# Reordering the stages of a recommendation-tower kernel: lookups three further ahead, small banks first in each quarter, 37 gathered rows, four one-hot chunks, and another place where gathers start

## The reference: what is computed

```python
e = jnp.stack([tbl_0[ids[:, 0]], ..., tbl_25[ids[:, 25]]], axis=1)
combined = jnp.concatenate([dense[:, None, :], e], axis=1)         # 2048 x 27 x 128
pairs = jnp.einsum('bfd,bgd->bfg', combined, combined)[:, I, J]    # upper triangle, 351
h = jnp.concatenate([dense, pairs, dense], axis=1)                 # 607
h = jnp.maximum(h @ W_top1 + b_top1, 0.0)                          # 512
h = jnp.maximum(h @ W_top2 + b_top2, 0.0)                          # 256
y = h @ W_top3                                                     # 1
```

## Time and profile before

| | |
|---|---|
| timed runs, median (lowest, highest) | 520.17 us (515.14, 522.70) |
| profiled execution, its own time | 515.3 us |
| its span, first to last instruction | 513.2 us |
| mean granted TensorE clock | 0.88 of full |
| TensorE matmul busy | 408.8 us, 80% of the span |
| VectorE, ScalarE busy | 262.7 us, 208.7 us |
| GpSimd busy | 254.1 us, 50% |

### The profile page before, as it was taken

The page is one execution under the profiler, slowest core; times in us unless marked ns, Lnnn a source line. Parts: engine busy times, 40 slices in busy tenths (PEclk is TensorE's granted clock), DMA queues, the critical chain, the costliest instruction groups (busy, mean ns, idle before and its releaser), DMA issues.

```text
span 513.2 us, 14192 instructions
## 1 busy us (share of the span) xinstructions
PE 408.8 (80%) x6280; PEld 365.9 (71%) x6280; DVE 262.7 (51%) x323; ACT 208.7 (41%) x436; POOL 254.1 (50%) x265
## 2 busy tenths in 40 slices
PE   5886727777978598875978788887989689789977
PEld 4776716767878497764967687785878588778755
DVE  3789505654555554663553655655364655454220
ACT  3456302234343543444342553435243543337432
POOL 5778875551555555552555535553555535540000
PEclk8998857776999898988897978997898969899989
DMA  6994251230322222221222212221232212210000
GB/s 170 227 240 107 67 158 50 70 108 23 74 59 78 56 64 68 69 64 32 64 66 70 63 49 64 67 74 49 68 68 69 63 42 70 58 39 1 4 1 0
DMA packets 27972, 36.34 MB, mean 71 GB/s; under 512 B 9151, under 2 KB 21959, under 8 KB 27912
## 3 DMA queue, kind: packets, MB, share of 16 engines
q1 hardware_dynamic: 19704, 18.65, 14.6%
q0 software_dynamic: 8192, 16.79, 13.5%
q10 hardware_dynamic: 16, 0.01, 0.0%
HBM read 35.42 MB, written 0.01 MB: 69 GB/s over the span
## 4 chain that ended last, share of the span: by engine, by line
PE 71%; issue 13%; ACT 4%; SPq 4%; DMA 4%; DVE 2%; another core or an unknown queue 1%; ACTq 0%; DVEq 0%
PE ring L411 17%; PE ring L412 15%; PE gram L449 10%; PE ring L485 8%; PE ring L431 7%; PE ring L494 6%; DMA dense<-in_r_dense_features 4%; PE ring L483 3%; SPq L281 2%; PE ring L461 2%; PE ring L472 2%; DVE pairs_and_more L674 2%; PE ring L503 2%; ACT pairs_and_more L578 1%; SPq L275 1%
## 5 line engine op out<-in xcount | busy, mean ns | idle before, releaser
L359 POOL DMA_INDIRECT rows<-in_tbl,ids_all x256 | 248.7, 971 | 201.1 <-PE gram L449 127.3
L651 DVE TENSOR_TENSOR onehot<-idb,vrow 125x1024 fp32r<-125x1024 f32 x160 | 192.7, 1222 | 130.5 <-PE ring L412 58.7
L411 PE MATMUL ring<-onehot,table_hi 125*128 125x256 f32 x608 | 181.6, 328 | 22.1 <-DVE pairs_and_more L674 7.6
L412 PE MATMUL ring<-onehot,table_lo 125*128 125x256 f32 x608 | 169.5, 309 | 0.0
L411 PEld LDWEIGHTS ring<-onehot,table_hi 125*128 125x128 f32 x608 | 132.9, 219 | 28.8 <-issue 8.7
L412 PEld LDWEIGHTS ring<-onehot,table_lo 125*128 125x128 f32 x608 | 133.4, 219 | 0.8
L559 ACT COPY xt<-ring 128x256 f32<-128x256 f32 x80 | 54.2, 677 | 128.9 <-PE ring L412 68.3
L449 PE MATMUL gram<-xt 128*27 128x26 f32 x4096 | 55.1, 201 | 42.6 <-issue 40.0
L449 PEld LDWEIGHTS gram<-xt 128*27 128x27 f32 x4096 | 47.8, 114 | 51.7 <-issue 46.0
L567 ACT COPY xt<-ring 128x512 f32<-128x512 f32 (+1 forms) x56 | 51.2, 987 | 24.1 <-remote 16.0
L431 PE MATMUL ring<-ident,rows 128*128 128x128 f32 x256 | 38.6, 285 | 13.6 <-issue 6.7
(11 more groups left out here) (41 smaller groups left out, 209.7 us busy)
## 6 DMA issues: line engine op xcount, KB each, us to landing
ids_spread<-in_ids_t SPq DMA_DIRECT2D x70, 128.0 KB
rows<-in_tbl,ids_all POOLq DMA_INDIRECT x256
xt<-in_tbl SPq DMA_DIRECT2D x6, 448.0 KB
w<-in_tbl SPq DMA_DIRECT2D x3, 448.0 KB
rows<-in_ids_t SPq DMA_DIRECT2D x10, 128.0 KB, 5.7
dense<-in_r_dense_features SPq DMA_DIRECT2D x16, 64.0 KB
w<-in_W_top SPq DMA_DIRECT2D x4, 256.0 KB
w<-in_W_top SPq DMA_DIRECT2D x1, 512.0 KB
```

Source lines behind the costliest of these rows:

```text
L359: pool.indirect_dma_start(rows[:, i % ROWS, :], None, aps[f"tbl_{f}"], bass.IndirectOffsetOnAxis(ap=ids_all[:, k, f:f + 1].bitcast(U32), a ...
L411: pe.matmul(ps, table_hi[:, m, c * KC + k, :], chosen, start=first, stop=False)
L412: last = pe.matmul(ps, table_lo[:, m, c * KC + k, :], chosen, start=False, stop=final)
L651: dve.tensor_tensor(onehot[:, (CH * u + c) % SLOTS], idb[0:VP, u % 2, 0:BS].unsqueeze(1).to_broadcast([VP, KC, BS]), vrow[:, c * KC:(c + 1 ...
```

## The change

The order of `stages()` is new. The lookups of block n + 1 now begin in the fourth quarter of block n - 1 (three of them), so they are three further ahead. Unblock and pairs of block n move out of its fourth quarter into the first two quarters of block n + 1, the layers follow them later, and the two tiles' rows are spread over the quarters with the first two banks of a next tile a quarter earlier. In each quarter the small banks stand ahead of most lookups. The copies of `gram` are a stage of their own ("grams"), with the engines exchanged. Pairs take two banks instead of three and layer 1 two instead of four. There are four one-hot slots in place of three, and VectorE makes one-hots one lookup further ahead; ScalarE lays out ids three ahead. `rows` has 37 places instead of 45, which is the same memory as the fourth slot. The rows of the first tile of a block are all stored by ScalarE.

A group of gathers from the fourth on waits for the bank that stands just ahead of a product step (`TURNS`), not for the end of the step before it. The two lower parts on GpSimd stand one group earlier. The first block's ids come in one DMA of ten rows and are spread by TensorE with a matmul (`spread_first_ids`); the first two dense tiles are loaded behind the fourth and the seventh table.

```diff
-ROWS = 45
+ROWS = 37
-    SLOTS = 3
+    SLOTS = 4
@@ stages()
+        yield "first_ids", 0, 0, 0
+        yield "first_ids", 0, 1, 0
+        for m in range(NL - 1):
+            if m + 2 < NL:
+                yield "first_ids", 0, m + 2, 0
+            yield from lookups(0, m)
+        yield from rows(0, 0, 0, 1, 2, 3, 4)
         yield from lookups(0, NL - 1)
         for n in range(NB):
             yield "products", n, 0, 0
+            yield from layer("unblock", n - 1, 0, 1)
+            yield from lookups(n + 1, *([0, 1, 2] if n == 0 else [3]))
+            yield from layer("unblock", n - 1, 2, 3)
+            yield "grams", n, 0, 0
+            yield from layer("layer3", n - 2, 0)
+            yield from rows(n, 1, 0, 1)
+            yield from lookups(n + 1, *([3] if n == 0 else [4, 5]))
+
+            yield "products", n, 1, 0
+            yield "grams", n, 1, 0
+            yield from layer("pairs", n - 1, 0, 1)
+            yield from lookups(n + 1, *([4, 5] if n == 0 else [6]))
+            yield from rows(n, 1, 2, 3, 4)
+            yield from layer("layer1", n - 1, 0)
+            yield from lookups(n + 1, *([6] if n == 0 else [7]))
+
+            yield "products", n, 2, 0
+            yield "grams", n, 2, 0
+            yield from layer("layer1", n - 1, 1)
+            yield from lookups(n + 1, *([7] if n == 0 else []))
+            yield from rows(n + 1, 0, 0, 1)
+            yield from lookups(n + 1, 8, 9)
+
+            yield "products", n, 3, 0
+            yield "grams", n, 3, 0
+            yield from layer("layer2", n - 1, 0)
+            yield from rows(n + 1, 0, 2, 3, 4)
+            yield from lookups(n + 2, 0)
             if n == NB - 1:
+                yield from layer("unblock", n, 0, 1)
+            yield from layer("layer2", n - 1, 1)
+            yield from lookups(n + 2, 1, 2)
+        yield from layer("unblock", NB - 1, 2, 3)
+        yield from layer("layer3", NB - 2, 0)
+        yield from layer("pairs", NB - 1, 0, 1)
+        yield from layer("layer1", NB - 1, 0, 1)
...
+    RING_ORDER = [stage for stage in stages() if stage[0] in RING_STAGES + ("products",)]
+    TURNS = [stage_ahead for stage_ahead, stage in zip(RING_ORDER, RING_ORDER[1:]) if stage[0] == "products"]
-        return g == 1 or (t, g) == (1, 3)
+        return t == 1 and g in (1, 3)
-    FIRST_GROUPS_BEHIND = {1: 0, 2: 3, 3: 6, 4: 9}
+    FIRST_GROUPS_BEHIND = {1: 0, 2: 3, 3: 6}
@@ SP
+            sp.dma_start(first_ids_i, aps["ids_t"][:, 0:BS]).then_inc(first_ids_landed, 16)
             for m in range(NL):
-                spread_ids(m)
                 load_raw(m)
-            load_dense(0)
-            load_dense(1)
+                if m in (3, 6):
+                    load_dense(m // 4)
@@ GpSimd
-                    pool.wait_ge(gram_ready, group - 4)
+                    pool.wait_ge(ring_filled, filled(*TURNS[group - 4]))
...
+                    if (k, g) == (1, GROUP):
+                        for m in LO_ON_GPSIMD:
+                            lower_part(m)
@@ TensorE
+            def spread_first_ids(m):
+                if m == 0:
+                    pe.wait_ge(first_ids_ready, 1)
+                if m >= 2:
+                    pe.wait_ge(onehot_ready, CH * (m - 1))
+                pe.matmul(idb[0:VP, m % 2, 0:BS], ident[0:NL, m:m + 1].to_broadcast([NL, VP]), first_ids, start=True,
+                          stop=True).then_inc(first_idb_ready, 1)
@@ VectorE
+                if s == 0 and n > 0:
+                    dve.wait_ge(ring_filled, filled("unblock", n - 1, NU - 1, 0))
                 dve.tensor_copy(*product_views(s)).then_inc(gram_dve, 1)
...
-                        one_hot(u, 0)
-                        ...
-                        one_hot(u, 1)
+                    if u + 1 < NB * NL:
+                        one_hot(u + 1, 0, 1)
```

More of the change, by code:

```diff
@@ L97, in stages @@
[L97 to L106, removed]
-            if n == NB - 1:
-                yield from layer("layer2", n - 1, 0)
-            yield "products", n, 2, 0
@@ L193, in build @@
         y_row = beside_pairs[:, 0:BS]
[L195 to L203, removed]
+        first_ids_i = pairs_and_more[0:NL, 0, 0:BS].bitcast(I32)
+        first_ids = pairs_and_more[0:NL, 1, 0:BS]
         W = KT * D
@@ L218, in build @@
         ids_landed = sem("ids_landed")
-        first_ids_landed = [sem(f"first_ids_landed{m}") for m in range(NL)]
+        first_ids_landed = sem("first_ids_landed")
+        first_ids_ready = sem("first_ids_ready")
+        first_idb_ready = sem("first_idb_ready")
         ids_spread_landed = [sem(f"ids_spread_landed{q}") for q in range(IDS_SLOTS)]
@@ L510, in _ @@
             for stage, n, a, b in stages():
-                if stage == "lookup":
+                if stage == "first_ids":
+                    spread_first_ids(a)
+                elif stage == "lookup":
                     lookup(n, a)
@@ L579, in store_unblocked, with store_pairs, store_layer1, store_layer2 @@
                 last.then_inc(left("unblock", n, b, 0), 1)
-            def store_pairs(n, k):
-                w = K_PAIR[k][1]
-                ps = bank("pairs", n, k, 0)
-                act.copy(x[0:w, k, :], ps[0:w, 0:BS]).then_inc(left("pairs", n, k, 0), 1)
-            def store_layer(stage, n, b, h_next, bias):
-                ps = bank(stage, n, b, 0)
-                act.activation(h_next[:, b, :], ps[:, 0:BS], ACT.Relu, bias=bias[:, b:b + 1]).then_inc(left(stage, n, b, 0), 1)
+            def store_pairs(n, b):
+                ps = bank("pairs", n, b, 0)
+                k, w = (slice(0, 2), P) if b == 0 else (slice(2, 3), K_PAIR[2][1])
+                act.copy(x[0:w, k, :].rearrange("p k s -> p (k s)"), ps[0:w, 0:(k.stop - k.start) * BS]).then_inc(
+                    left("pairs", n, b, 0), 1)
+            def store_layer1(n, b):
+                ps = bank("layer1", n, b, 0)
+                for i in range(2):
+                    block = 2 * b + i
+                    last = act.activation(h1[:, block, :], ps[:, i * BS:(i + 1) * BS], ACT.Relu, bias=b1[:, block:block + 1])
+                last.then_inc(left("layer1", n, b, 0), 1)
+            def store_layer2(n, b):
+                ps = bank("layer2", n, b, 0)
+                act.activation(h2[:, b, :], ps[:, 0:BS], ACT.Relu, bias=b2[:, b:b + 1]).then_inc(left("layer2", n, b, 0), 1)
             def store_y(n):
@@ L603, in _ @@
             act.copy(x[:, 0, 0:P], ident[:])
+            act.wait_ge(first_ids_landed, 16)
+            act.copy(first_ids, first_ids_i).then_inc(first_ids_ready, 1)
             act.wait_ge(pads_cleared, 1)
-            for m in (0, 1):
-                lay_out_ids(m)
-                upper_part(m)
+            upper_part(0)
+            upper_part(1)
             for stage, n, a, b in stages():
                 if stage == "lookup":
-                    if n * NL + a + 2 < NB * NL:
-                        lay_out_ids(n * NL + a + 2)
+                    if NL <= n * NL + a + 3 < NB * NL:
+                        lay_out_ids(n * NL + a + 3)
                     if n == 0 and a + 2 < NL:
@@ L616, in _ @@
                     store_rows(n, a, b)
-                elif stage == "products" and a % 2 == 0:
+                elif stage == "grams" and a % 2 == 1:
                     store_products(n, a)
@@ L699, in _ @@
                     store_unblocked(n, a)
-                elif stage == "products" and a % 2 == 1:
+                elif stage == "grams" and a % 2 == 0:
                     store_products(n, a)
```

102 lines of the change are left out of this document (38 added, 64 removed).

## The result

| | before | after |
|---|---|---|
| timed runs, median (lowest, highest) | 518.75 us (515.14, 522.70), 4 runs | 753.30 us (752.83, 754.25), 4 runs |
| ratio, 95% interval | | 1.457 (1.450 to 1.464) |
| profiled execution, its span | 515.3, 513.2 us | 754.25, 752.4 us |
| TensorE busy; mean granted clock | 408.8 us, 80%; 0.88 | 512.0 us, 68%; 0.76 |

The changed kernel is 46% slower; the forecast was 445 us, range 412 to 495. Times depend on the chip: on the chip of this comparison, and on two chips of later runs, the kernel before took about 520 us, on three others 404 to 408. None of the later chips was met a second time, so whether a chip always belongs to its kind, or was only in a state of that kind, is not shown.

A forecast was written before the change was run, and what follows sets the result against it. The prediction took TensorE's order and its unexplained idle time, with product steps stalled by gathers, as the bound. First block 105, six blocks 291 and last 45 made 441 us of span; 445 us predicted, range 412 to 495.

The forecast's parts named there:

- The step that failed: Product step starting with a group of gathers: expected to get through undisturbed, 1.2 us inside a quarter of 11.6 us.
- the drain: Behind a group's last gather issue: product step goes on 1.6 us later; rival with 2.5 us gave 462, chance 0.10.
- The work of the quarters: A block's four quarters: 12.4 us for the first with VectorE, then 10.5, 9.4 and 11.6 of TensorE work.
- The unblock chain: Unblock, copies and pairs at a block's end: now costs nothing, with lookups and the product step between its banks.
- The ring of 37: Places for gathered rows, 37 instead of 45: costs nothing; a late transpose would cost its lateness, at most a quarter.
- ScalarE's copies: Storing the first tile's second bank on ScalarE: 1.2 us hidden in idle time; without that cover 1.2 us a block.
- The end: Last block, without lookups: 42.69 us before plus 2.5 us of unblock and pairs, taken as 45 us.
- The start: Before the first product step: 6 us saved (bounds 2 and 9), so it comes at 44 instead of 50.5 us.
- the spread matmuls: Ten small matmuls spreading the first block's ids: no cost counted, since they lie beside table loads.
- The last line of the sum: Whole kernel: 441 us span plus 2.1 is 443; timed median was 4.9 us above the profiled execution; put at 445.
- Slower by merged groups: Rival: gather groups follow without a gap twice a block, product steps wait over 10 us; 573 us, chance 0.07.
- all slower cases: Chance that the change makes the kernel slower, from two merges or one merge with a worse first block: 0.08.

The follow-up runs named there:

- h4: Changed kernel with the old wait, product steps in pairs and 16 gathers behind each pair; 638.11 us, ratio 1.237 to the kernel before.
- i4: Changed kernel unedited, on a chip where the kernel before took 403.82 us; 409.98 us, ratio 1.019.
- f4: Changed kernel with each gather replaced by a plain DMA of the same 64 KB issued by GpSimd; 384.53 us.
- h1: Changed kernel with the old wait: gathers wait for the end of a product step; 478.97 us, ratio 0.927 where the kernel before took 520.4 us.

## Why the prediction was wrong

**The step that failed** is this one: "The step that starts with the group should get through: eight gathers begin with 0.95 us of issue, and the lookup and layer bank directly behind 184.11 ran undisturbed". With it the step's 1.2 us stood inside a quarter of "0.3 + 9.7 + 1.6 = 11.6 us". The step stalls within 0.6 us, and since it now begins with the group instead of ending ahead of it, it waits out all 9.7 us plus the drain: 12.4 us, which then stand in front of the quarter's other 10 to 13 us. The evidence was misread. I took the undisturbed lookup and bank as a sign that the start of a group is harmless. A lookup starts 32 instructions in 2.1 us, a product step 256 in 1.2. What those rows showed was that this work asks for little, and `h4` shows that even lookups starve when the stock is gone. My own rule, "a product step can't finish while gathers are in flight", already forbade the exception, and the earlier trace rows showed it at work: the step at 60.49 began with gathers beside it, thirteen of the 16 still to be issued, the first of them 0.04 us behind its start, did 40 matmuls and stood still, as the 28 steps here do after 46. I had used that row for the drain alone. Two rows of the timeline before, the issue beside that step and TensorE's next portion:

```profile
60.53 0.95 POOL L359 DMA_INDIRECT rows<-in_tbl,ids_all  x1 [0.30 <-issue]
...
61.23 0.25 PE L449 MATMUL gram<-xt 128*27 128x26 f32 x5 [0.21 <-issue]
```

**The account.** The prediction had 105 + 291 + 45 = 441 us of span; measured are 142.4 to the first step of block 1, 567.4 for six blocks (94.6 each), 42.6 at the end, 752.4. Against the same kernel on the second kind of chip (`i4`), block 2 is 95.99 instead of 46.30 us. The steps are 49.6 of it against 8.2, so 41.4 us are stalls. The rest is 46.4 against 38.2: 8.2 us, at half clock for a part of each quarter (a mean granted clock of 0.79 to 0.86 in the four rests of block 1) against 1.00. The six blocks, 567.4 against 270.7 us, are 297 of the 344 us between the two spans; the first block has 45, its four steps starved likewise, and the start 3.

**Right.** The drain: 1.66 and 1.68 us, as forecast (1.6). It isn't without exception: in the kernel before, the step at 50.48 went on 0.37 us behind an issue. The last gather of the group at 142.76 begins at 151.52 and its last packet ends 2.26 us later; TensorE goes on 0.35 us after that. The Trainium skill, "DMA: Bandwidth & Descriptors", section on the anatomy of a GpSimd-issued DMA, has 2.0 us fixed and so 2.15 us for 64 KB by my estimate. Counted from the begin of the issue, the trace roughly agrees; the prediction set this figure against 1.6 us, which counts from the issue's end. So the step does seem to wait until the last gather has landed, and that is what the 1.6 us contain. The work of the quarters: forecast 12.4, 10.5, 9.4, 11.6 without waits, in `i4` 12.18, 11.44, 10.33, 12.35 with steps 0.8 us longer. The unblock chain costs nothing (the unblock bank starts at 154.76, directly behind the step). The ring of 37 and ScalarE's copies cost nothing that shows. The end: 42.6 us for 45. The order itself: 7% with the old wait, on the first kind.

**Mis-sized.** The start: the first step came at 56.6 us, not 44, later even than the 50.5 before. I had put the spread matmuls at nothing, "beside table loads". They are 20 at 519 ns, 8.4 us of TensorE, which is busy 47.6 us before its first step instead of 37.2:

```profile
L397 PE MATMUL idb<-pairs_and_more,ident 10*125 10x256 f32 x20 | 8.4, 519 | 3.8 <-issue 3.8
```

They explain only a part. `f4` has the same 20 matmuls (8.1 us), and its first step comes at 47.6: 3.6 us of the 12.6 stay without indirect DMAs, and 9.0 go with them, by which path wasn't looked into.

With the old wait (`h1`) blocks 1 to 6 on the first kind take 48.8 to 58.2 us, 53.8 on the mean, not 48.5. In most of them the third and fourth step begin beside the last gathers of a group or just behind them and wait out the drain (2.5 to 4.8 us each), and GpSimd then waits for them. The last line of the sum, 443 and 4.9 us for the median, makes 448 and not the 445 that I put; it changes nothing here.

**The rivals.** Slower by merged groups had the right sign (573 us) and the right sight, a step that waits over 10 us, but for another reason: groups don't merge here, GpSimd waits 10 to 16 us between them. What was missing is the plain rival "the step does not get through". By my own rows it was 0.3 + 9.7 + 1.6 = 11.6 us of step in front of some 10 of work, four times a block: 87 us and over 650 in all. I put together no such sum, and gave 0.08 to all slower cases.

**What stays open.** How the indirect DMAs cut TensorE off, and why two chips of one type differ. That it is instructions that TensorE lacks is itself inferred: "issue" only says that it waits for nothing the profile shows. The first portion was 46 matmuls in nearly every starved step, but since the group starts 0.34 us behind the step, that number may be the stock or the moment of the cut. The instruction fetches in the page of the profile are 50 packets of 16 KB, 0.5% of the DMA engines' span, so their bytes are no load. The kept trace has their times: 0.9 to 1.8 us each, 0.9 to 1.9 in `f4`. In 9 of the 28 starved steps none starts, and in no step more than one. At the step at 142.42 one ends at 142.49 and the next starts at 155.79, and in between eleven small portions and the burst arrive. So the portions are not these fetches, and the gathers don't slow them. The waits behind a long burst look different: in `h4`, TensorE stops at 206.00, a packet runs from 206.49 to 207.41, and it goes on at 208.73. The Trainium skill, "Runtime: NRT & Kernel Launch", section on instruction fetch mechanics, says that an engine streams its instructions in 16 KiB blocks by its own DMA queue and that the cost is mostly hidden. The block size agrees with the profile's packets. Behind that burst the cost would not be hidden, if the 2.74 us are a wait for the packet; the 224 us in the starved steps are something else.

## What to carry to other kernels

Before moving work beside indirect DMAs, count the instructions a us that it asks for, not its busy time: on the first kind of chip, work that asks for 16 ran beside a group of eight, work that asks for 200 stopped. Put instruction-dense stages (many small matmuls) where no gather has been issued for 2 us, and don't double a group: beside 16 gathers even lookups ran dry. How long a gap between groups has to be wasn't measured. Time such a change on more than one chip. And when the rows give a rule ("can't finish while gathers are in flight"), let the exception that the plan needs be a rival with its own sum.

## What the runs showed of the hardware that I had not expected

- Beside indirect DMAs issued by GpSimd TensorE waits without a visible reason, as if short of instructions: a step of 256 took 12.4 us beside eight of them. Plain DMAs from GpSimd with the same bytes and packets, and GpSimd's own compute, left it at 1.27 us on the same chip.
- The stop comes 0.24 us after the first issue begins and 1.6 us before the first packet; the end comes 0.2 to 0.5 us behind the last packet.
- The size differs by chip: 12.4 us on one kind, 2.0 on the other; the changed kernel 753 and 410 us, the kernel before 520 and 405. Two kernels without indirect DMAs took nearly the same, one on each (385.74 us by SP on the second kind, 384.53 by GpSimd on the first); neither was run on both.
- What TensorE can still do runs out: beside the first eight of 16 gathers 133 instructions started, beside the second eight 17; and without gathers 484 in one burst were followed by 2.74 us of nothing.
